# Last part of a vision tower: the first layer of each block with the tokens on the partitions, and four transpositions a step

## The chip, the cores and the metric

The kernel runs on one core of a Trainium2 chip. The core has five engines with a queue of their own each, which meet only through semaphores: TensorE (PE; its weight loads are shown as PEld), VectorE (DVE), ScalarE (ACT), GpSimd (POOL) and SyncE (SP), which only issues DMAs here. The metric is the device time of one execution in microseconds (us).

## The reference

A vision tower with 1,216 tokens of 256 features, in the kernel ten tiles of 128 tokens (the last is half full): patch embedding, attention, a mixture of experts, an integer attention, and last a residual network of three blocks. Only the last is touched:

```python
h = x
for blk in range(3):
    i0, i1 = (2 * blk, 2 * blk + 1)
    y = _qlora_linear(h, qweights[i0], scales[i0], biases[i0], lora_a[i0], lora_b[i0])
    y = _layernorm(y, ln_gamma[blk], ln_beta[blk])
    y = jax.nn.gelu(y, approximate=False)
    y = _qlora_linear(y, qweights[i1], scales[i1], biases[i1], lora_a[i1], lora_b[i1])
    h = y + h
```

`_qlora_linear` is `x @ w.T + bias` with a 256x256 matrix in float32 (the low rank term is added into it earlier), and `_layernorm` takes the mean off, divides by the root of the variance over the 256 features of a token, and applies gamma and beta.

## The kernel before

All of it is one program with every instruction and every wait written out; nothing is reordered. The last part (`ffn_tensor`, `ffn_scalar`, `ffn_vector`, `ffn_pool`) runs 15 steps: three blocks of five chunks, four chunks of 256 tokens and one of 192 (the short chunk, steps 4, 9 and 14). Step n is chunk n % 5 of block n // 5. Ahead of the steps, tiles of normed tokens are turned by TensorE (`turned`, L2323) and copied to SBUF by ScalarE (`entered`, L2400) into `ffn_xT`, which holds the features on the partitions; tiles 4 to 9 are interleaved with steps 0 to 2.

The weights of the first layer have been centred along their outputs, so that the mean of y is taken off by the product, and the bias likewise. A step before the change:

- `first` (PE, L2337): four products into `psum`, outputs on the partitions, tokens along the row.
- `squared` (ACT): two squares (L2410) and two copies with bias (L2412) out of `psum`, into `ffn_sq` and `ffn_y`.
- `joined` (DVE, L2266): adds the two halves of the squares.
- `summed` (PE, L2346): two products with a column of ones add up the squares over the partitions.
- `variance` (DVE, L2261), then a power of -1/2 on GpSimd (L2311) into `ffn_rs`.
- `spread` (PE, L2354): two products put that factor, one for each token, on all partitions.
- `normed` (DVE, L2273): multiplies y by it. `gelu` (ACT, L2420): two Gelus with gamma and beta.
- `second` (PE, L2370; in the last block L2376 and L2378, which end with the tokens on the partitions), and `added` (DVE, L2282; in the last block L2289, L2291 and L2292), which adds the residual.

In steps 5 to 9 GpSimd also adds the last bias to `h` (L2314), right behind its power. The order on TensorE is i = 0, 1, 2, ...: `first(i)`, (while i < 3: two `turned`), `summed(i-1)`, `spread(i-2)`, `second(i-3)`. In float32 one product of the program is two MATMUL instructions in the trace, a transposition is one. Names in the rows are memory regions: `ring` holds `ffn_y` and `ffn_sq`, `experts` holds the weights and `ffn_xT`, `tab` the identity and the ones, `shared` the last bias.

## Time and profile before

| | |
|---|---|
| time, median of 3 runs | 561.8 us (560.23 to 562.18) |
| the profiled execution's own time, and its span | 560.42 us, 558.6 us |
| busy in the span: PE, PEld, DVE, ACT, POOL | 419.3, 308.4, 317.6, 247.1, 143.7 us |
| mean granted TensorE clock | 0.841 of 2.4 GHz |
| the 15 steps on PE (first L2337 to last L2378) | 483.2 to 555.0 us |

The span is from the first to the last instruction; the execution's time lies 1.8 us above it. "Busy" adds up instructions; what an engine's idle time costs is told by the chain of work that ended last. The granted clock of TensorE is 1.00 (2.4 GHz) or 0.50 (1.2 GHz) in a stretch.

### The profile page before, as it was taken

The page shows a single profiled execution, that of the slowest core. Times are in us where ns is not written, and L with a number is a line of the kernel's source. Part 1 is how long each engine was busy: PE and PEld are TensorE (multiplying, and loading weights), DVE is VectorE, ACT ScalarE, POOL GpSimd, SP SyncE. Part 2 cuts the span into 40 slices and gives each one's busy share as a digit, 9 for nine tenths or more (in the row PEclk, how much of TensorE's full clock was granted, in tenths as well). Part 3 has the DMA queues.
Part 4 walks back from the last instruction along what each step waited for, and adds up shares of the span by engine and source line. Part 5 has one row for each costly group of instructions (what it writes and reads, how often), then busy time and mean ns, then how long its engine had stood idle before and what let it go on. Part 6 is the DMA issues. An engine that isn't in the chain of part 4 may idle for free.

```text
span 558.6 us, 9536 instructions
## 1 busy us (share of the span) xinstructions
PE 419.3 (75%) x3508; PEld 308.4 (55%) x3509; DVE 317.6 (57%) x867; ACT 247.1 (44%) x518; POOL 143.7 (26%) x169
## 2 busy tenths in 40 slices
PE   4777785468778999999889994632794235799997
PEld 3545562246568885666555793321442233589996
DVE  3858875489855421223311128669898975645642
ACT  4235543336656411222222212693396665385661
POOL 3644443069911240000000054008010001113410
PEclk9969987559999999999999998575556555599999
DMA  8921111096004222111101071000000000000002
GB/s 296 404 105 19 17 18 19 14 397 284 4 1 193 84 101 86 48 47 39 58 19 39 29 287 51 0 1 3 2 0 0 2 5 1 2 0 1 1 19 72
DMA packets 19793, 38.64 MB, mean 69 GB/s; under 512 B 2136, under 2 KB 16164, under 8 KB 18340
## 3 DMA queue, kind: packets, MB, share of 16 engines
q1 hardware_dynamic: 18788, 35.41, 18.3%
q0 software_dynamic: 960, 2.62, 1.4%
q8 instruction: 29, 0.48, 0.4%
q14 instruction: 16, 0.13, 0.1%
HBM read 29.77 MB, written 7.01 MB: 66 GB/s over the span
## 4 chain that ended last, share of the span: by engine, by line
PE 52%; DVE 24%; ACT 10%; issue 6%; POOL 6%; DMA 1%; SPq 0%; DVEq 0%; ACTq 0%
PE psum L1255 11%; PE psum L1262 6%; PE psum L1287 5%; PE psum L2337 4%; PE psum L1301 3%; PE psum L2370 3%; POOL ring L782 3%; POOL experts L787 2%; PE psum L610 2%; PE psum L2376 2%; PE psum L1279 1%; ACT experts L1663 1%; PE psum L2354 1%; DMA experts<-in_tern 1%; DVE ring L1939 1%
## 5 line engine op out<-in xcount | busy, mean ns | idle before, releaser
L1255 PE MATMUL psum<-experts,ring 128*128 x136 | 64.3, 596 | 1.9 <-issue 1.2
L1079 DVE TENSOR_TENSOR ring<-ring,psum 128x512 f32<-128x512 f32 x17 | 11.7, 688 | 62.8 <-PE psum L1255 62.8
L1186 POOL DMA_INDIRECT front<-expert_results,slot_of x10 | 9.9, 992 | 125.0 <-DMA expert_results<-ring 122.2
L1262 PE MATMUL psum<-front,shared 128*128 128x256 f32 (+1 forms) x160 | 34.6, 370 | 0.0
L1255 PEld LDWEIGHTS psum<-experts,ring 128*128 128x128 f32 x136 | 23.3, 190 | 19.4 <-issue 19.4
L1287 PE MATMUL psum<-experts,ring 128*128 x136 | 32.1, 379 | 0.0
L1287 PEld LDWEIGHTS psum<-experts,ring 128*128 128x128 f32 x136 | 25.8, 190 | 10.3 <-issue 7.6
L1262 PEld LDWEIGHTS psum<-front,shared 128*128 128x128 f32 x160 | 29.2, 190 | 3.2
L1385 ACT COPY ring<-psum 128x512 f32<-128x512 f32 x17 | 10.0, 586 | 42.3 <-PE psum L1279 42.3
L2337 PE MATMUL psum<-experts 128*128 128x256 f32 (+1 forms) x120 | 28.6, 384 | 0.0
L590 PE MATMUL psum<-experts,ring 128*128 128x256 f32 x108 | 25.9, 391 | 0.4 <-DVE experts L485 0.4
L1371 ACT COPY ring<-psum 128x256 f32<-128x256 f32 x17 | 6.3, 372 | 42.8 <-PE psum L1271 42.8
L782 POOL TENSOR_TENSOR ring<-ring,att_max 128x608 f32<-128x608 f32 x16 | 19.3, 1209 | 20.0 <-DVE att_max L849 19.2
L2337 PEld LDWEIGHTS psum<-experts 128*128 128x128 f32 x120 | 23.0, 200 | 2.7
L814 PE MATMUL psum<-tab,experts 128*128 128x128 f32 x128 | 18.8, 295 | 7.5 <-ACT ring L876 7.4
L1301 PE MATMUL psum<-shared,ring 128*128 128x256 f32 (+1 forms) x80 | 20.0, 406 | 4.5 <-issue 4.5
L618 PE MATMUL psum<-tab,ring 128*128 128x128 f32 x30 | 6.7, 343 | 22.0 <-DVE ring L451 22.0
L590 PEld LDWEIGHTS psum<-experts,ring 128*128 128x128 f32 x108 | 20.8, 199 | 3.7 <-DVE experts L485 0.6
L2111 POOL TENSOR_TENSOR rstd<-out_var,minus_half 128x2 f32<-128x2 f32 x5 | 4.2, 832 | 70.5 <-DVE out_var L2091 70.5
L2311 POOL TENSOR_TENSOR ffn_rs<-ffn_var,minus_half 128x2 f32<-128x2 f32 x15 | 10.4, 693 | 45.2 <-DVE ffn_var L2261 45.2
L2410 ACT ACTIVATE ring<-psum,ffn_first_b 128x256 f32<-128x256 f32 (+1 forms) x30 | 12.3, 459 | 20.5 <-PE psum L2337 20.5
L610 PE MATMUL psum<-qkv_w,ring 128*128 128x384 f32 x40 | 20.4, 647 | 1.1 <-DVE qkv_w L496 1.1
(364 smaller groups left out, 1076.0 us busy)
## 6 DMA issues: line engine op xcount, KB each, us to landing
experts<-in_experts SPq DMA_DIRECT2D x8, 1536.0 KB, 12.8
experts<-in_x SPq DMA_DIRECT2D x9, 384.0 KB, 8.2
expert_rows<-zeros SPq DMA_DIRECT2D x1, 2176.0 KB, 15.0
ring<-expert_rows SPq DMA_DIRECT2D x17, 128.0 KB, 2.1
shared<-in_shared SPq DMA_DIRECT2D x1, 1536.0 KB, 18.1
experts<-in_ffn_q SPq DMA_DIRECT2D x1, 1536.0 KB
experts<-in_ffn_s SPq DMA_DIRECT2D x1, 1536.0 KB
experts<-in_pos_embed SPq DMA_DIRECT2D x1, 1152.0 KB, 8.7
```

The source lines that it names most:

```text
L590: mm = nc.tensor.matmul(psum[:, Y, 0:D], tok_xT[t % 2][:, k, :], patch_c[:, k, :], start=(k == 0), stop=(k == KP - 1))
L610: mm = nc.tensor.matmul(psum[:, Z, 0:QKV], qkv_hT[t % 2][:, k, :], qkv_w[:, k, :], start=(k == 0), stop=(k == KD - 1))
L782: nc.gpsimd.tensor_tensor(att_s[p % 3], att_s[p % 3], m, ALU.subtract).then_inc(s_shifted.sem, 1)
L814: tr = nc.tensor.transpose(psum[:, 4 + c // 4, (c % 4) * P:(c % 4 + 1) * P], att_p[p % 3][:, 2 * c:2 * c + 2, :], ident)
L1079: nc.vector.tensor_tensor(o, o, up_bank(g), ALU.mult).then_inc(hidden_done.sem, 1)
L1255: mm = nc.tensor.matmul(bank, sl_xT[t % 2][:, k, :], slot_w(t, block, k, F), start=(k == 0), stop=(k == KD - 1))
L1262: mm = nc.tensor.matmul(o[:, b, 0:w], shared_w(block, k, (2 * half + b) * P, P), moe_x(c)[:, k, 0:w], start=(k == 0), stop=(k == KD - 1))
L1287: mm = nc.tensor.matmul(psum[:, 2, 0:D], sl_hT[t % 2][:, k, :], slot_w(t, 2, k, D), start=(k == 0), stop=(k == KF - 1))
L1301: mm = nc.tensor.matmul(psum[0:m, 3, u * D:(u + 1) * D], sh_h[c % 2][:, k, u * P:u * P + m], shared_w(2, k, 0, D), start=(k == 0), stop=(k ...
L2337: mm = nc.tensor.matmul(psum[:, n % 2, o * CHUNK:o * CHUNK + w], ffn_w[:, 2 * b, k, o * P:(o + 1) * P], ffn_xT[:, k, a:a + w], start=(k == ...
L2370: mm = nc.tensor.matmul(psum[:, 6 + n % 2, o * CHUNK:o * CHUNK + w], ffn_w[:, 2 * b + 1, k, o * P:(o + 1) * P], g[:, k, 0:w], start=(k == ...
L2410: nc.scalar.activation(ffn_sq[n % 2][:, k, 0:w], psum[:, n % 2, k * CHUNK:k * CHUNK + w], ACT.Square, bias=ffn_first_b[:, b, k:k + 1])
```

## The change

The first layer is computed with the tokens on the partitions, so that the squares of a token add up along its row. Line numbers of the changed kernel differ by some 10 to 20.

- `first` (now L2356): the tokens are the stationary side, and the 256 outputs the moving one, in all chunks.
- `biased` (new, DVE, L2277): adds a centred bias row, out of `psum` into `ffn_yt`, 128 x 512 at once (two instructions for the short chunk).
- `squared` (ACT, L2417): one Square of each tile out of `ffn_yt`, with its sum along the row.
- `variance` (DVE, L2285) adds the epsilon only; the power on GpSimd stays.
- `normed` (DVE, L2291): one multiplication of each tile by its column of `ffn_rs`, in SBUF.
- `y_turned` (new, PE, L2367): four transpositions into `psum`. `gelu` (ACT, L2427) reads them there.
- `joined`, `summed`, `spread` and the two copies with bias are gone.
- The pipeline has a stage less: `first(i)`, `y_turned(i-1)`, `second(i-2)`.
- Three bias rows are fetched behind the last bias (SP), and GpSimd takes the mean off them (L1882) behind the two memsets at L1874 and L1875.

```diff
+            for b in range(FFN_BLOCKS):
+                sp.dma_start(ffn_rows[:, b, :], ins["ffn_rows"][2 * b:2 * b + 1, :].to_broadcast((P, D))).then_inc(l_ffn_last.sem, 16)
...
+            pool.wait_ge(ffn_bias_ready.sem, ffn_bias_ready.done(0))
+            pool.wait_ge(l_ffn_last.sem, l_ffn_last.all)
+            for b in range(FFN_BLOCKS):
+                w = nc.gpsimd.tensor_scalar(ffn_rows[:, b, :], ffn_rows[:, b, :], ffn_mean[:, b:b + 1], None, ALU.add)
...
+            def biased(n):
+                dve.wait_ge(ffn_first.sem, ffn_first.done(n))
+                if n >= 3:
+                    dve.wait_ge(ffn_y_turned.sem, ffn_y_turned.done(n - 3))
+                z = psum[:, n % 2, :].rearrange("p (u d) -> p u d", u=2)
+                for m, u in parts(n):
+                    w = nc.vector.tensor_tensor(ffn_yt[n % 3][0:m, u, :], z[0:m, u, :],
+                                                ffn_rows[0:m, n // NC:n // NC + 1, :].to_broadcast((m, u.stop - u.start, D)), ALU.add)
...
             def normed(n):
-                w = FFN_CHUNKS[n % NC][1]
-                y = ffn_y[n % 4][:, :, 0:w]
-                dve.wait_ge(ffn_spread.sem, ffn_spread.done(n))
-                rs = psum[:, 4 + n % 2, 0:w].rearrange("p (o c) -> p o c", o=1).to_broadcast((P, KD, w))
-                nc.vector.tensor_tensor(y, y, rs, ALU.mult).then_inc(ffn_normed.sem, 1)
+                dve.wait_ge(ffn_rs_ready.sem, ffn_rs_ready.done(n))
+                for u, (_, m) in enumerate(tiles_of_chunk(n % NC)):
+                    y = ffn_yt[n % 3][0:m, u, :]
+                    w = nc.vector.tensor_scalar(y, y, ffn_rs[0:m, n % 2, u:u + 1], None, ALU.mult)
+                w.then_inc(ffn_normed.sem, 1)
...
-            for i in range(STEPS + 4):
-                if 0 <= i - 4 < STEPS:
-                    added(i - 4)
-                if 0 <= i - 1 < STEPS:
-                    variance(i - 1)
-                if 0 <= i - 2 < STEPS:
-                    normed(i - 2)
+            for i in range(STEPS + 3):
+                if 0 <= i - 3 < STEPS:
+                    added(i - 3)
+                if 0 <= i - 1 < STEPS:
+                    normed(i - 1)
                 if i < STEPS:
-                    joined(i)
+                    biased(i)
+                    variance(i)
...
-                for o in range(KD):
+                for u, (t, m) in enumerate(tiles_of_chunk(c)):
                     for k in range(KD):
-                        mm = nc.tensor.matmul(psum[:, n % 2, o * CHUNK:o * CHUNK + w], ffn_w[:, 2 * b, k, o * P:(o + 1) * P], ffn_xT[:, k, a:a + w],
+                        mm = nc.tensor.matmul(psum[0:m, n % 2, u * D:(u + 1) * D], ffn_xT[:, k, t * P:t * P + m], ffn_w[:, 2 * b, k, :],
...
+                        tr = nc.tensor.transpose(bank[:, k, u * P:u * P + m], ffn_yt[n % 3][0:m, u, k * P:(k + 1) * P], ident[0:m, 0:m])
...
+                    y = nc.scalar.activation(ffn_sq[n % 2][0:m, u, :], ffn_yt[n % 3][0:m, u, :], ACT.Square, scale=D ** -0.5, accum_out=ffn_mean_sq[0:m, n % 2, u:u + 1])
...
-            for i in range(STEPS + 2):
+            for i in range(STEPS + 1):
                 if i < STEPS:
                     squared(i)
                 if i < 3:
                     entered(4 + 2 * i)
                     entered(5 + 2 * i)
-                if 0 <= i - 2 < STEPS:
-                    gelu(i - 2)
+                if 0 <= i - 1 < STEPS:
+                    gelu(i - 1)
```

The semaphores of this part are those of earlier parts under new names, and the order shows the old ones: `gate_done` is `ffn_first`, `sl_hT_ready` is `ffn_rs_ready`, `sl_y_ready` is `ffn_normed`, `sh_down` is `ffn_gelu`, `sh_added` is `ffn_second`, `sl_hidden_turned` is `ffn_xT_ready`, `sl_xT_ready` is `ffn_turned`, `silu_done` is `ffn_squared`, `hidden_done` is `ffn_var_ready`, and `sl_down` is `ffn_spread` before and `ffn_y_turned` in the changed kernel.

TensorE before, from the end of `first(3)` to `first(4)`:

```order
L2337 MATMUL psum<-experts 128x256 x3
L2346 MATMUL psum<-tab,ring 128x1 [waits hidden_done,ffn_joined]
L2346 MATMUL psum<-tab,ring 128x1
L2354 MATMUL psum<-tab,ffn_rs 128x128 [waits sl_hT_ready]
L2354 MATMUL psum<-tab,ffn_rs 128x128
L2370 MATMUL psum<-ring,experts 128x256 [waits sl_hidden_turned,sh_down]
L2370 MATMUL psum<-ring,experts 128x256 x3
L2337 MATMUL psum<-experts 128x192 [waits silu_done,sl_hidden_turned]
L2337 MATMUL psum<-experts 128x192 x3
```

And TensorE in the changed kernel, from `y_turned(1)` to the first half of `first(4)`:

```order
L2367 MATMUL psum<-tab,ring 128x128 [waits sl_y_ready]
L2367 MATMUL psum<-tab,ring 128x128 x3
L2382 MATMUL psum<-ring,experts 128x256 [waits sl_hidden_turned,sh_down]
L2382 MATMUL psum<-ring,experts 128x256 x3
L2356 MATMUL psum<-experts 128x256 [waits ffn_biased,sl_hidden_turned]
L2356 MATMUL psum<-experts 128x256 x3
L2367 MATMUL psum<-tab,ring 128x128 [waits sh_down,sl_y_ready]
L2367 MATMUL psum<-tab,ring 128x128 x3
L2382 MATMUL psum<-ring,experts 128x256 [waits sl_hidden_turned,sh_down]
L2382 MATMUL psum<-ring,experts 128x256 x3
L2356 MATMUL psum<-experts 128x256 [waits ffn_biased,sl_hidden_turned]
L2356 MATMUL psum<-experts 128x256
```

`second(0)` (L2370, now L2382) stood ahead of `first(4)` and stands ahead of `first(3)` now; between two steps there is one wait on VectorE's result where there were two.

VectorE in a step of the changed kernel, from `variance(n-1)` to `biased(n)`:

```order
L2285 TENSOR_SCALAR ffn_var<-ffn_mean_sq 128x2 [waits sl_hT_ready,silu_done]
L2301 SCALAR_TENSOR_TENSOR experts<-psum,ffn_cols,experts 128x256 [waits sh_added]
L2301 SCALAR_TENSOR_TENSOR experts<-psum,ffn_cols,experts 128x256
L2291 TENSOR_SCALAR ring<-ring,ffn_rs 128x256 [waits sl_hT_ready]
L2291 TENSOR_SCALAR ring<-ring,ffn_rs 128x256
L2277 TENSOR_TENSOR ring<-psum,shared 128x512 [waits sl_down,gate_done]
```

`normed` waits for GpSimd's power of the same step, stands behind `added` of two steps earlier, and `biased` stands behind it.

ScalarE while the steps start, in the changed kernel, from `entered(4)` and `entered(5)` (L2410) to `squared(2)` and `entered(8)`:

```order
L2410 COPY experts<-psum 128x2x128 [waits sl_xT_ready] x2
L2417 ACTIVATE ring,ffn_mean_sq<-ring 128x256 [waits ffn_biased]
L2417 ACTIVATE ring,ffn_mean_sq<-ring 128x256
L2410 COPY experts<-psum 128x2x128 [waits sl_xT_ready] x2
L2427 ACT_TABLE_LOAD
L2427 ACTIVATE ring<-psum,ffn_cols 128x256 [waits sl_down]
L2427 ACTIVATE ring<-psum,ffn_cols 128x256
L2417 ACTIVATE ring,ffn_mean_sq<-ring 128x256 [waits hidden_done,ffn_biased]
L2417 ACTIVATE ring,ffn_mean_sq<-ring 128x256
L2410 COPY experts<-psum 128x2x128 [waits sl_xT_ready] x2
```

The copies of tiles 8 and 9 now stand behind `gelu(0)`; before, they stood ahead of it.

## Rows read from the trace of the kernel before

**Rows 1.** Chain that ended last, a step in steady state: start us, us, what

```profile
519.08 1.30 PE psum L2337 x8
520.38 0.34 PE psum L2346 x4
520.72 0.55 PE psum L2354 x4
521.27 1.73 PE psum L2370 x8
523.00 1.73 PE psum L2337 x8
```

**Rows 2.** The same chain, while the steps start

```profile
486.72 0.44 PE psum L2323 x4
...
493.76 1.28 ACT L2420
...
496.20 1.99 PE psum L2370 x8
```

**Rows 3.** Timeline, PE's next group and `added` behind a `second`

```profile
501.95 1.89 PE L2337 MATMUL psum<-experts 128*128 128x256 f32 x8
502.16 0.88 DVE L2282 SCALAR_TENSOR_TENSOR experts<-psum,ffn_cols,experts 128x256 f32<-128x256 f32 x2 [0.77 <-PE psum L2370]
```

**Rows 4.** Timeline, DVE and POOL in one step (start us, us, [idle before <-releaser])

```profile
525.10 0.16 DVE L2261 TENSOR_SCALAR ffn_var<-psum 128x2 f32<-128x2 f32 x1 [1.17 <-PE psum L2346]
525.34 0.69 POOL L2311 TENSOR_TENSOR ffn_rs<-ffn_var,minus_half 128x2 f32<-128x2 f32 x1 [2.41 <-DVE ffn_var L2261]
...
525.65 0.69 DVE L2273 TENSOR_TENSOR ring<-ring,psum 128x512 f32<-128x512 f32 x1 [0.40 <-PE psum L2354]
525.99 1.27 POOL L2314 TENSOR_TENSOR h<-h,shared 128x512 f32<-128x512 f32 x1
526.37 1.18 DVE L2266 TENSOR_TENSOR ring<-ring 128x256 f32<-128x256 f32 x1
```

**Rows 5.** ACT: timeline at 407.7 us, then groups by line (busy, mean ns)

```profile
407.72 0.36 ACT L2226 ACTIVATE experts<-psum 128x256 f32<-128x256 f32 x1
407.98 0.19 ACT L2226 ACTIVATION_READ_ACCUMULATOR experts<-psum 128x1 f32 x1
...
L2234 ACT ACTIVATE experts<-experts,lora_mean 128x256 f32<-128x256 f32 x5 | 2.1, 495 | 0.0
```

**Rows 6.** Timeline, DVE, an earlier part of the kernel

```profile
259.05 0.61 DVE L1500 TENSOR_SCALAR front<-front,w_inv 128x256 f32<-128x256 f32 x2
```

**Rows 7.** Timeline, ACT and DVE behind `first(0)`

```profile
486.76 0.84 ACT L2410 ACTIVATE ring<-psum,ffn_first_b 128x256 f32<-128x256 f32 x2 [2.77 <-PE psum L2337]
...
487.05 0.73 DVE L2098 TENSOR_SCALAR ring<-h,hst,rstd 128x256 f32<-128x256 f32 x2 [1.42 <-PE psum L2323]
...
488.20 0.66 ACT L2400 COPY experts<-psum 128x256 f32<-128x256 f32 x2
488.36 0.42 DVE L2266 TENSOR_TENSOR ring<-ring 128x256 f32<-128x256 f32 x1 [0.57 <-ACT ring L2412]
```

**Rows 8.** Timeline, POOL and DVE at 377 us

```profile
376.96 1.73 POOL L2242 TENSOR_SCALAR experts<-experts 128x512 f32<-128x512 int32 x2 [28.24 <-ACT experts L1723]
...
377.05 1.17 DVE L1646 TENSOR_SCALAR front<-experts 128x1152 bf16<-128x1152 f32 x1
```

**Rows 9.** Stretches: us, busy PE PEld DVE ACT POOL, granted clock, DMA share, GB/s

```profile
63.07:66.48 3.41, 1.80 (x9) 1.22 (x10) 3.16 (x16) 1.14 (x3) 1.00 (x2) 1.00 0.20 19
...
69.90:73.31 3.41, 1.36 (x7) 0.96 (x7) 3.12 (x17) 1.06 (x4) 0.55 (x1) 1.00 0.28 30
73.31:76.72 3.41, 3.41 (x12) 2.58 (x11) 2.60 (x9) 2.78 (x9) 2.63 (x5) 0.50 0.02 5
```

**Rows 10.** Timeline, PE in the stretch at 69.9 us

```profile
72.03 0.55 PE L618 MATMUL psum<-tab,ring 128*128 128x128 f32 x3 [2.05 <-DVE ring L451]
```

**Rows 11.** Timeline, POOL behind its memsets

```profile
468.06 0.81 POOL L2111 TENSOR_TENSOR rstd<-out_var,minus_half 128x2 f32<-128x2 f32 x1 [57.35 <-DVE out_var L2091]
```

More of the change, by code:

```diff
@@ L1429, in tower @@
         ffn_last = view(shared, 0, D)
+        ffn_rows = view(shared, D, FFN_BLOCKS, D)
         ffn_q = view(experts, 0, 3072).bitcast(I32)
@@ L2176, in tower @@
         ffn_mean = sb("ffn_mean", [P, B])
-        ffn_first_b = sb("ffn_first_b", [P, B, KD])
+        ffn_mean_sq = sb("ffn_mean_sq", [P, 2, 2])
+        ffn_yt = [view(ring, 4096 + u * 2 * D, 2, D) for u in range(3)]
         lora_sum = sb("lora_sum", [P, B, KD])
@@ L2257, in variance @@
             def variance(n):
[L2258 removed]
+                dve.wait_ge(ffn_squared.sem, ffn_squared.done(n))
                 if n >= 2:
                     dve.wait_ge(ffn_rs_ready.sem, ffn_rs_ready.done(n - 2))
[L2261 to L2266 removed]
@@ L2333, in first, with y_turned @@
                 if n >= 2:
-                    pe.wait_ge(ffn_squared.sem, ffn_squared.done(n - 2))
-                for o in range(KD):
+                    pe.wait_ge(ffn_biased.sem, ffn_biased.done(n - 2))
+                for u, (t, m) in enumerate(tiles_of_chunk(c)):
                     for k in range(KD):
-                        mm = nc.tensor.matmul(psum[:, n % 2, o * CHUNK:o * CHUNK + w], ffn_w[:, 2 * b, k, o * P:(o + 1) * P], ffn_xT[:, k, a:a + w],
+                        mm = nc.tensor.matmul(psum[0:m, n % 2, u * D:(u + 1) * D], ffn_xT[:, k, t * P:t * P + m], ffn_w[:, 2 * b, k, :],
                                               start=(k == 0), stop=(k == KD - 1))
                 mm.then_inc(ffn_first.sem, 1)
-            def summed(n):
-                pe.wait_ge(ffn_joined.sem, ffn_joined.done(n))
+            def y_turned(n):
+                pe.wait_ge(ffn_normed.sem, ffn_normed.done(n))
                 if n >= 2:
-                    pe.wait_ge(ffn_var_ready.sem, ffn_var_ready.done(n - 2))
-                for u in range(2):
-                    mm = nc.tensor.matmul(psum[:, 2 + n % 2, u:u + 1], ffn_sq[n % 2][:, 0, u * P:(u + 1) * P], ones[:, 0:1], start=True, stop=True)
-                mm.then_inc(ffn_summed.sem, 1)
-            def spread(n):
-                pe.wait_ge(ffn_rs_ready.sem, ffn_rs_ready.done(n))
-                if n >= 2:
-                    pe.wait_ge(ffn_normed.sem, ffn_normed.done(n - 2))
+                    pe.wait_ge(ffn_gelu.sem, ffn_gelu.done(n - 2))
+                bank = psum[:, 4 + n % 2, :].rearrange("p (k c) -> p k c", k=KD)
                 for u, (_, m) in enumerate(tiles_of_chunk(n % NC)):
-                    mm = nc.tensor.matmul(psum[:, 4 + n % 2, u * P:u * P + m], ffn_rs[:, n % 2, u:u + 1].to_broadcast((P, P)), ident[:, 0:m],
-                                          start=True, stop=True)
-                mm.then_inc(ffn_spread.sem, 1)
+                    for k in range(KD):
+                        tr = nc.tensor.transpose(bank[:, k, u * P:u * P + m], ffn_yt[n % 3][0:m, u, k * P:(k + 1) * P], ident[0:m, 0:m])
+                tr.then_inc(ffn_y_turned.sem, 1)
             def second(n):
@@ L2383, in ffn_tensor @@
                 turned(t)
-            for i in range(STEPS + 3):
+            for i in range(STEPS + 2):
                 if i < STEPS:
@@ L2390, in ffn_tensor @@
                 if 0 <= i - 1 < STEPS:
-                    summed(i - 1)
+                    y_turned(i - 1)
                 if 0 <= i - 2 < STEPS:
-                    spread(i - 2)
-                if 0 <= i - 3 < STEPS:
-                    second(i - 3)
+                    second(i - 2)
         def ffn_scalar(act):
```

48 lines of the change are left out of this document (22 added, 26 removed).

## The prediction

> **What bounds the kernel now.** I read the chain of work that ended last first. From 498.2 us to the end of the last product it is TensorE alone, product behind product: a full step is `summed` 0.34, `spread` 0.55, `second` 1.73 and `first` 1.73 us, 4.35 together; in the short chunk `first` and `second` take 1.30 each [rows 1]. In the last block `second` is longer, and the chain is TensorE's just the same. So in these 57 us every microsecond of TensorE counts, and the other engines have slack. Before 498.2 the steps fill up: TensorE waits once, some 0.8 us, for ScalarE's table load (1.28) and first Gelus, and `second(0)` starts at 496.20 [rows 2]. The reader is to see that the change takes work from the bounding engine, and lengthens the loop that runs through the others.
>
> **TensorE's work.** Removed: 15 `summed` at 0.34 = 5.1, and 15 `spread` at 0.55 (some 0.50) = 8.1; together 13.2. Added: 15 times four transpositions. The same operation on the same shape is there: four in 0.44 [rows 2]; 12 full steps and 3 short ones at 0.33 make 6.3. `first` of the short chunk now moves 256 outputs for two tiles, 1.73 for 1.30, three times: 1.3. **Net -5.6 us.** If TensorE stayed the bound throughout, that would be the result.
>
> **The new chain of one step**, from the last product of `first(n)` to the first transposition of `y_turned(n)`:
>
> to VectorE: 0.20 from the start of TensorE's next group to an operation behind a product [rows 3]
>
> `biased`: 0.69, as the other sum of 128x512 out of `psum` [rows 4]; 0.04 on to ScalarE
>
> two squares with their accumulator reads: the trace has no such pair out of SBUF. Below: the pair out of `psum` (the read starts 0.26 behind its operation, the next operation 0.10 later: 0.36 apart; then 0.26 + 0.19) gives 0.81 [rows 5]. Above: two of 0.495 end to end with two reads of 0.19 give 1.37. An SBUF operation of 256 takes 0.495 against 0.36 [rows 5], overlapped as that pair: 0.49 to the second start, then 0.39 + 0.19: **1.07**
>
> 0.04, `variance` 0.16, 0.08 to 0.17 on to GpSimd (525.10 + 0.16 to 525.34), power 0.69 [rows 4], 0.10 back to VectorE (my estimate, between the hand-overs of 0.04 and 0.17)
>
> `normed`: 0.61 for two, the second 0.27 behind the first, as the two multiplications of 128x256 by a column [rows 6]; 0.05 to TensorE.
>
> That is 3.82. On TensorE there stand between the same two points `y_turned(n-1)` 0.44, `second(n-2)` 1.73, `first(n+1)` 1.73: 3.90. So in steady state without disturbance the chain is just hidden. The other loop is hidden as closely: behind a `second`, VectorE needs 0.20, `added` 0.81 to its release (0.88 less the overlap) [rows 3], `normed` 0.61 and 0.05, 1.67 against the 1.73 of the `first` that stands between. Before, two hand-overs with separate slots shared this latency, and VectorE never had more than 1.2 us of it in one slot.
>
> **Where it isn't hidden**, in four places, and the clock.
>
> *The start.* By hand, from the moment VectorE is free at 487.7 (487.05 + 0.73) [rows 7]: `biased(0)` to 488.4, where ScalarE read `psum` directly at 486.76 [rows 7]. Squares to 489.5; the copies of tiles 4 and 5 (0.66 for two [rows 7]) stand behind them, so `turned(6)` starts at 489.9: TensorE, done with `first(1)` and nothing else to do since 488.7, idles 1.1. The rest of the chain ends at 491.3: 1.0 idle before `y_turned(0)`. `first(2)` to 493.5. `biased(1)` 491.2, squares to 493.0, copies 6 and 7 to 493.6; `y_turned(1)` at 494.8: 0.9 idle. ScalarE goes on in its order: table load 1.28 to 494.8 [rows 2], `gelu(0)` some 1.0 (two operations of 0.5, as the one in SBUF [rows 5]) to 495.9, squares(2) to 496.9, copies 8 and 9 to 497.5, and `second(0)` waits for tile 9: it starts at 497.5, after 2.3 idle. Sum 5.3 against 0.8: **+4.5**. `second(0)` starts 1.3 later than before, with one `first` less done.
>
> *Steps 5 to 9.* GpSimd starts its 1.27 us addition as the power ends (525.99 against 525.34 + 0.69), and `joined`, issued at 526.37, ends at 527.55 [rows 4], though it takes 0.42 where GpSimd is idle [rows 7]: it began about 1.14 behind GpSimd's start. `joined` reads two tensors in SBUF. `normed` reads one, but a one-tensor operation was held too: 1.17 us for 1152 elements beside GpSimd [rows 8]. Now `normed` is released by just that power, so each of the five comes up against the addition. From the start of `biased` to the next: 0.69 + 0.04 + 1.07 + 0.04 + 0.16 + 0.17 + 0.69 = 2.86, then 1.10 held, then 0.53 to issue `normed`: 4.49 for a step, against 3.90. The first of them is late by 0.9 (3.82 + 1.10 less the 3.90), four by 0.6, and the one that has the short `second(4)` beside it by 0.4 more: 3.7; with `biased` in two pieces in step 9 (0.1), **+3.8**. That makes these steps slower than before (4.35), not quicker.
>
> *The end.* `normed(14)` stands behind `added(12)`, and no `first` hides it any more: 0.20, 0.62 for the sum (0.69 [rows 4] less the overlap), 0.61 and 0.05 = **+1.5** idle. Before, this slot was full.
>
> *The rest.* Behind `second(9)`, 0.43 shorter than a full one, the chain of 3.82 sticks out by 0.35, and each idle time adds about 0.1 to load weights (1.99 against 1.73 includes that and the last product's latency [rows 1, 2]) where it is not itself inside a longer loop: **+0.6**.
>
> Sum: -5.6 + 4.5 + 3.8 + 1.5 + 0.6 = **+4.8**.
>
> *The clock.* Nearly all of the last part runs at 2.4 GHz. Between 493.5 and 497.5 TensorE would have only two transpositions of tiles and `y_turned(1)`, 0.7 to 0.9 us of work around an idle time of 2.3. In 69.90 to 73.31 it was busy 1.36 us, and ran at 1.2 GHz from 73.31 to 76.72; in 63.07 to 66.48, busy 1.80, it kept 2.4 [rows 9]. The first of these held an idle time of 2.05 [rows 10]. The new start is nearer to the first. A stretch as long as that one at half speed, TensorE being busy in 2.6 us of it, costs 1.3; a second one costs 1.7 more. I take **+2.7**, with 0 and 3.5 as bounds.
>
> Hidden: the three bias rows' DMAs go out behind the last load of SyncE before the outputs, and nothing on it waits for them in between. GpSimd's three sums (up to 0.6 each, as L2242 [rows 8]) fit into the 57.35 us it idles behind its memsets [rows 11]; a hold on VectorE by them, were it not covered, would cost at most 1.8. VectorE's and ScalarE's totals fall and bound nothing.
>
> The profiled execution took 560.42: 560.4 + 4.8 + 2.7 = 567.9. The median of the runs stands 1.4 higher, so I say **568.3 us**.
>
> **The rivals.**
>
> *The clock stays* (0.25). 560.4 + 4.8 = 565.2. For it: TensorE is never idle for more than 2.3 us in one piece at the start, and it kept its clock behind a stretch in which it was idle for 1.6 of 3.4 us [rows 9]. Against it: it has less work here than in either. The Trainium skill (TensorE: Matmul & The Clock Gate, section "HAM oscillation — how this bites in real kernels") ties the fall to an idle gap of TensorE that by its figure is longer than any worked out here; by that rule the clock stays, and the time is this rival's. The trace disagrees with the rule: the fall at 73.31 came behind an idle time of 2.05 us.
>
> *`normed` is not held by GpSimd* (0.15). 3.8 goes: 564.1 with the fall, 561.4 without. Against it: the operation at 377.05 [rows 8], a single case with another output type. The Trainium skill (SBUF — State Buffer, section "Who interferes with whom") describes a port that the two engines lock against each other; by it `normed` is held and this rival is out.
>
> *Faster* (0.05): the chain through ScalarE is much shorter than I size it, and TensorE stays the bound. The place is the pair of squares and all that waits on it: three of the idle times at the start and the hold in steps 5 to 9 (which is inside a loop with the squares). Each 0.1 us less for the pair saves about 0.9 in all; at the lower end, 0.81, the sum is +2.4, and 562.8 without the fall of the clock. It decides for faster from 0.23 for the pair on (4.8 less 7.6 is -2.8, 557.6 us); the trace has no single ScalarE operation of 256 elements under 0.36 [rows 5].
>
> *Slower still* (0.10): squares at 1.37, +2.7 more, or the clock falls a second time at the end: 570.5 to 573.
>
> The likeliest as worked out: 0.45, own range 566.5 to 570.
>
> **How the numbers follow.** 0.5% (2.8 us) is about what a measurement of this kernel can tell from no change. Slower by more: the likeliest, the clock rival (+4.8), the slower one, and the held-free case with the fall (+3.7): 0.45 + 0.25 + 0.10 + 0.10, less 0.06 for mis-sizing, 0.84. Within: the held-free case without the fall and that 0.06: 0.11. Faster: 0.05. The range leaves out the faster case, the held-free one without the fall and the end of the slowest: 562.5 to 572.5.
>
> **What would show it.** In the profile of the changed kernel: `y_turned` at 0.44 and no more; idle of TensorE before L2367 put down to VectorE, in steps 5 to 9 about 0.6 to 1.0 each and almost none in steps 2 to 4; L2291 at 1.4 to 1.7 us for two in steps 5 to 9 and 0.61 elsewhere; L2382 first at 497.5, released by ScalarE's copy; a granted clock of 0.50 just behind; 1.5 idle before the last L2367. I am wrong if steps 5 to 9 are 3.9 long, if the start is shorter, or if the pair of squares isn't near 1.07.

## The result, and the profile after

The changed kernel took **564.6 us** (median of 17 runs, 561.5 to 569.1) against 560.4 for the one before (17 runs, 556.1 to 562.2): ratio 1.0090, 95% interval 1.0060 to 1.0119. Taken again (12 runs) it was 1.0051, 1.0022 to 1.0080. By the two ratios it is slower by 2.9 and 5.0 us, by their intervals by 1.2 to 6.7. The profiled execution took 561.69 us, with a span of 559.9 and a mean granted clock of 0.857. Of the profiles below, that of "last norm first" is of a slow execution (568.45 us, the kernel's median is 560.9), so only the rows of its last part are used, and not its time.

Of the page after, the row of busy times (419.3 on PE before, 143.7 on POOL, 247.1 on ACT):

```profile
PE 414.5 (74%) x3449; PEld 298.2 (53%) x3449; DVE 319.7 (57%) x885; ACT 235.0 (42%) x518; POOL 146.6 (26%) x172
```

TensorE does less, as the change means it to, and the kernel takes longer. (Part of the 4.8 us is the clock: the row of `first(0)`, which ran at the lower clock for a while, is 3.35 us before and 2.16 here.) VectorE's total is not smaller but larger, 319.7 for 317.6. The chain of work that ended last says why: while the steps start it is ScalarE's rows above all, and in steps 5 to 9 VectorE's stand in it, where [rows 1] are TensorE alone.

```profile
486.27 0.92 ACT ring L2417 x4
490.97 1.28 ACT L2427
493.18 0.90 ACT ring L2417 x4
494.76 1.97 PE psum L2382 x8
...
509.85 0.98 DVE ring L2291 x2
511.53 1.32 PE psum L2382 x8
513.53 1.10 DVE ring L2291
```

Timeline of PE while the steps start, in steps 5 and 6, and at the end (start us, us, [idle before <-releaser]); it answers to [rows 2]:

```profile
482.42 2.16 PE L2356 MATMUL psum<-experts 128*128 128x256 f32 x8
...
487.58 0.69 PE L2342 MATMUL psum<-tab,ring 128*128 128x128 f32 x4 [0.84 <-ACT experts L2410]
488.95 0.66 PE L2367 MATMUL psum<-tab,ring 128*128 128x128 f32 x4 [0.68 <-DVE ring L2291]
...
492.10 0.66 PE L2367 MATMUL psum<-tab,ring 128*128 128x128 f32 x4 [0.33 <-DVE ring L2291]
494.76 1.97 PE L2382 MATMUL psum<-ring,experts 128*128 128x256 f32 x8 [2.00 <-ACT experts L2410]
...
510.87 0.66 PE L2367 MATMUL psum<-tab,ring 128*128 128x128 f32 x4 [0.21 <-DVE ring L2291]
...
515.04 0.66 PE L2367 MATMUL psum<-tab,ring 128*128 128x128 f32 x4 [0.48 <-DVE ring L2291]
...
550.01 0.70 PE L2367 MATMUL psum<-tab,ring 128*128 128x128 f32 x4 [1.30 <-DVE ring L2291]
```

The waits stand at the start, in steps 5 to 9 and at the end, where the prediction put them, with the releasers that it gave them; in steps 7 and 8 no idle time is listed. Two things help in reading such rows. A full group whose row is 1.89 is followed by the next one 1.73 after its start where nothing is waited for. So a row reaches 0.16 into its follower, and an idle time in brackets begins 0.16 late: the 2.00 is 2.16. And lengths are best taken from start to start.

One chain of a step, timeline of ACT, DVE and POOL behind `first(0)`, where nothing else is in the way; it answers to [rows 4, 5, 7]:

```profile
486.27 0.42 ACT L2417 ACTIVATE ring<-ring 128x256 f32<-128x256 f32 x1 [3.24 <-DVE ring L2277]
486.60 0.19 ACT L2417 ACTIVATION_READ_ACCUMULATOR ring<-ring 128x1 f32 x1
486.69 0.40 ACT L2417 ACTIVATE ring<-ring 128x256 f32<-128x256 f32 x1
486.99 0.19 ACT L2417 ACTIVATION_READ_ACCUMULATOR ring<-ring 128x1 f32 x1
...
487.21 0.17 DVE L2285 TENSOR_SCALAR ffn_var<-ffn_mean_sq 128x2 f32<-128x2 f32 x1 [0.97 <-ACT ring L2417]
...
487.55 0.69 POOL L2330 TENSOR_TENSOR ffn_rs<-ffn_var,minus_half 128x2 f32<-128x2 f32 x1 [3.04 <-DVE ffn_var L2285]
...
488.27 0.62 DVE L2291 TENSOR_SCALAR ring<-ring,ffn_rs 128x256 f32<-128x256 f32 x2 [0.89 <-POOL ffn_rs L2330]
```

The pair of squares takes 0.91 (486.27 to 487.18).

And step 5, where GpSimd adds the last bias:

```profile
508.48 0.69 POOL L2330 TENSOR_TENSOR ffn_rs<-ffn_var,minus_half 128x2 f32<-128x2 f32 x1 [3.30 <-DVE ffn_var L2285]
...
508.98 0.87 DVE L2301 SCALAR_TENSOR_TENSOR experts<-psum,ffn_cols,experts 128x256 f32<-128x256 f32 x2 [0.57 <-PE psum L2382]
...
509.13 1.27 POOL L2333 TENSOR_TENSOR h<-h,shared 128x512 f32<-128x512 f32 x1
509.77 1.05 DVE L2291 TENSOR_SCALAR ring<-ring,ffn_rs 128x256 f32<-128x256 f32 x2
```

`normed` takes 1.05 for 0.61. It began 0.64 behind the addition, since `added` stood ahead of it on VectorE. In the five steps it takes 1.05, 1.45, 0.90, 1.02 and 1.09.

**One length for all kernels below** is that of the last part, from the start of `first(0)` to the end of the last product. The clock rises to 1.00 somewhere in `first(0)` or just ahead of it, differently in each execution: its row is 1.89 to 3.56 long, and that alone is worth up to 1.7 us. So I take off what the row of `first(0)` has over the 1.89 of a full one ("at full clock"). Before: 483.37 to 555.00, 71.6, with 3.35 for `first(0)`: **70.2**. After: 482.42 to 556.28, 73.9, with 2.16: **73.6**. The change costs 3.4 us there. The correction is good to some 0.2 us: in the second profile of the changed kernel the row of `first(0)` is 1.89, and its last part, less a fall of the clock told below, is 73.8. There `biased(0)` (485.63) stood behind VectorE's last multiplications of tokens (484.34 and on, without idle time), so that an earlier end of `first(0)` won nothing.

### The profile page after: what moved, and what is told of

Read it like the earlier page. It is cut to its first block, busy times and chain, and to the rows that moved or that the text cites. A ratio compares the mean times of both kernels' runs of the same rounds, so it can differ in the third digit from the quotient of the medians.

```text
span 559.9 us, 9452 instructions
## 1 busy us (share of the span) xinstructions
PE 414.5 (74%) x3449; PEld 298.2 (53%) x3449; DVE 319.7 (57%) x885; ACT 235.0 (42%) x518; POOL 146.6 (26%) x172
## 4 chain that ended last, share of the span: by engine, by line
PE 52%; DVE 27%; ACT 10%; issue 7%; POOL 2%; DMA 1%; SPq 0%; DVEq 0%; POOLq 0%; ACTq 0%
PE psum L1257 11%; PE psum L1264 6%; PE psum L1289 5%; PE psum L1303 3%; PE psum L2382 3%; PE psum L2356 3%; PE psum L2222 2%; PE psum L2221 2%; DVE ring L846 2%; DVE att_den L853 2%; PE psum L2388 2%; PE psum L610 1%; PE psum L2367 1%; PE psum L1281 1%; DVE att_max L849 1%
## 5 line engine op out<-in xcount | busy, mean ns | idle before, releaser
L1264 PE MATMUL psum<-front,shared 128*128 128x256 f32 (+1 forms) x160 | 36.1, 381 | 0.0
L1264 PEld LDWEIGHTS psum<-front,shared 128*128 128x128 f32 x160 | 30.4, 198 | 3.5
L2356 PE MATMUL psum<-experts 128*128 128x256 f32 (+1 forms) x120 | 29.1, 383 | 0.0
L2417 ACT ACTIVATE ring<-ring 128x256 f32<-128x256 f32 (+1 forms) x30 | 12.2, 408 | 36.1 <-DVE ring L2277 36.1
L2356 PEld LDWEIGHTS psum<-experts 128*128 128x128 f32 (+1 forms) x120 | 21.8, 188 | 3.9 <-issue 1.0
L1084 DVE TENSOR_TENSOR ring<-ring,psum 128x512 f32<-128x512 f32 (+1 forms) x10 | 6.6, 660 | 25.4 <-PE psum L1264 25.2
```

The lines of the kernel that those rows point to most:

```text
L1264: mm = nc.tensor.matmul(o[:, b, 0:w], shared_w(block, k, (2 * half + b) * P, P), moe_x(c)[:, k, 0:w], start=(k == 0), stop=(k == KD - 1))
L2356: mm = nc.tensor.matmul(psum[0:m, n % 2, u * D:(u + 1) * D], ffn_xT[:, k, t * P:t * P + m], ffn_w[:, 2 * b, k, :], start=(k == 0), stop=(k ...
L2417: y = nc.scalar.activation(ffn_sq[n % 2][0:m, u, :], ffn_yt[n % 3][0:m, u, :], ACT.Square, scale=D ** -0.5, accum_out=ffn_mean_sq[0:m, n % ...
```

## The experiments

| kernel | last part as it ran | at full clock | ratio to before (95%) |
|---|---|---|---|
| before, twice | 71.6, 71.6 | 70.2, 70.2 | 1 |
| changed, twice | 73.9, 75.5 | 73.6, 73.8 (fall taken off) | 1.0090 and 1.0051 |
| addition early | 72.1 | 71.7 | 1.0058 (1.0024 to 1.0091) |
| copies first | 74.0 | 72.3 | 1.0046 (1.0013 to 1.0080) |
| second later | 74.4 | 73.0 | 1.0036 (1.0001 to 1.0071) |
| last norm first | 75.3 | 72.5 (fall taken off) | 1.0030 (0.9997 to 1.0063) |
| three edits together | 70.8 | 69.3 | 1.0012 (0.9980 to 1.0045) |
| more room | 71.6 | 71.2 | 1.0016 (0.9978 to 1.0053) |
| third square | 76.6 | 76.1 | 1.0111 (1.0060 to 1.0161) |
| one stage more | 67.4 | 67.0 | 0.9937 (0.9905 to 0.9969) |
| and the table early | 66.5 | 66.1 | 0.9917 (0.9885 to 0.9950) |
| and full tiles | 65.8 | 65.3 | 0.9907 (0.9876 to 0.9937) |

Each ratio is to the runs of the kernel before that were taken beside it. The intervals are 3 to 4 us wide, that of the third square (4 runs) 5.7. Single edits are told apart by the profiles, and only the larger sums by the times.

### The changed kernel again, and the clock

> The changed kernel once more, to see whether its profile repeats and as the reference for the kernels beside it. Both theories of the clock: if the fall at the start that was predicted belongs to the kernel, a second profile shows a granted clock of 0.50 somewhere in 486 to 502 us and the time of this run is 2 to 3 us above 561.7; if it doesn't (or depends on the execution), the start runs at 1.00 as in the first profile, the idle times before second(0) are again 0.8, 0.7, 0.3, 2.0, and the kernel stays 3 to 5 us slower than the one before.

The idle times were there again, and this time the clock fell. Stretches (us, busy PE PEld DVE ACT POOL, granted clock), then PE's timeline:

```profile
492.18:495.59 3.41, 1.40 (x8) 1.12 (x9) 0.72 (x2) 3.40 (x11) 0.69 (x1) 1.00 0.00 0
495.59:499.00 3.41, 3.41 (x10) 2.69 (x9) 1.08 (x4) 0.04 (x1) 0.00 (x0) 0.50 0.00 0
```
```profile
494.85 3.03 PE L2382 MATMUL psum<-ring,experts 128*128 128x256 f32 x8 [2.00 <-ACT experts L2410]
497.67 2.55 PE L2356 MATMUL psum<-experts 128*128 128x256 f32 x8
500.06 0.60 PE L2367 MATMUL psum<-tab,ring 128*128 128x128 f32 x4
```

From the start of `second(0)` to `y_turned(2)` it is 5.21 us for 3.53: the fall costs 1.7. It is the fall that was predicted, in the stretch where it was put. Of the five profiles whose start is that of the changed kernel (both of its own, addition early, last norm first, more room) it came in two, here and in "last norm first" (3.43 for `second(0)`, +1.5), while every one of the five has the idle time of 2.00. So it depends on the execution. My estimate from these five is 0.6 us on average (1.7 and 1.5, divided by five), not 2.7; two falls in five are too few for more than that. The kernel before, looked at a second time, has its idle time of 0.66 ahead of `second(0)` again, and a granted clock of 1.00 from there to the end, as in its first profile.

### The addition early

```diff
             for n in range(STEPS):
+                if NC <= n < 2 * NC:
+                    pool.wait_ge(ffn_first.sem, ffn_first.done(n))
+                    nc.gpsimd.tensor_tensor(h[...], h[...], ffn_last..., ALU.add)
                 pool.wait_ge(ffn_var_ready.sem, ffn_var_ready.done(n))
...
-                if NC <= n < 2 * NC:
-                    nc.gpsimd.tensor_tensor(h[...], h[...], ffn_last..., ALU.add)
```

> In steps 5 to 9 GpSimd's addition now runs beside biased and squares, not beside normed. Theory (normed is held by GpSimd's addition): L2291 goes from 0.90 to 1.45 for two back to 0.61, the five steps go from 4.17 to 4.37 down to 3.9 to 4.05, and the time falls by 1.2 to 2.2 us against the changed kernel; biased may be held a little instead, by at most 0.3 in a step. Rival (the five steps are long because the chain through ScalarE is longer than TensorE's work): L2291 changes, the steps keep 4.1 to 4.3, time within 0.5 us.

DVE and POOL in step 5 of it:

```profile
509.37 0.60 DVE L2291 TENSOR_SCALAR ring<-ring,ffn_rs 128x256 f32<-128x256 f32 x2
510.30 0.69 DVE L2277 TENSOR_TENSOR ring<-psum,shared 128x512 f32<-128x512 f32 x1 [0.34 <-PE psum L2357]
```
```profile
510.34 1.27 POOL L2330 TENSOR_TENSOR h<-h,shared 128x512 f32<-128x512 f32 x1 [1.43 <-PE psum L2357]
```

`normed` is back at 0.60 to 0.62 in all five steps, and no idle time of TensorE is left in them. The period ahead of `y_turned(5)` is 4.13 against 4.50, and those from it on are 3.52, 3.95, 4.13, 3.95 and 4.13, against 4.17, 4.17, 4.29, 4.37 and 4.19 (3.9 to 4.05 were expected; the short chunks scatter them). The last part is 1.9 shorter. `biased`, which now begins beside the addition, takes 0.69 as ever: it reads `psum` and one tensor in SBUF. In the time the difference can't be seen (1.0058).

### The copies first

```diff
-                if i < STEPS:
-                    squared(i)
                 if i < 3:
                     entered(4 + 2 * i)
                     entered(5 + 2 * i)
+                if i < STEPS:
+                    squared(i)
```

> ScalarE copies tiles 4 to 9 ahead of the squares of steps 0 to 2. Theory (second(0) is late because ScalarE's copy of tile 9 stands behind three pairs of squares): the idle of 2.0 before the first L2382 shrinks to 0.9 to 1.2, where gelu(0) bounds it, and TensorE reaches the end 0.7 to 1.3 us earlier, less up to 0.6 that y_turned(0) and y_turned(1) lose because their squares now stand behind copies: 0.3 to 1.0 us faster than the changed kernel. Rival (the start is bound by the table load and gelu(0), whatever the copies do): second(0) within 0.2 us of where it was, no gain.

```profile
491.15 0.66 PE L2367 MATMUL psum<-tab,ring 128*128 128x128 f32 x4 [1.77 <-DVE ring L2291]
...
494.31 0.66 PE L2367 MATMUL psum<-tab,ring 128*128 128x128 f32 x4 [0.34 <-DVE ring L2291]
495.65 1.97 PE L2382 MATMUL psum<-ring,experts 128*128 128x256 f32 x8 [0.68 <-ACT experts L2410]
```

The 2.00 ahead of `second(0)` is 0.68, and the last part is 1.3 shorter, both beyond what was expected (0.9 to 1.2, and 0.3 to 1.0). It was the copy of tile 9 behind the squares. `y_turned(0)` and `y_turned(1)` lost nothing by the copies ahead of their squares: less the excess of `first(0)`, `y_turned(0)` starts 6.26 us after `first(0)` in both kernels, and `y_turned(1)` 3.16 after that (3.15 in the changed kernel).

### Second later

```diff
-                if 0 <= i - 2 < STEPS:
-                    second(i - 2)
+                if 0 <= i - 3 < STEPS:
+                    second(i - 3)
```
(TensorE; `added(i - 4)` on VectorE)

> second and added move one step later, so that first(3) stands ahead of second(0) again, as in the kernel before, and one more slot stands between the last y_turned and the last second. Theory (the missing stage costs the idle time at the start and at the end): the 2.0 before the first L2382 is filled by first(3), the step at the end keeps at most 0.7 of the 1.3 idle before the last L2367; sum 1.5 to 2.5 us faster than the changed kernel. Rival (the order with more distance only shifts the idle time: first(5) then waits for added(0), which now comes one step later): an idle time of 0.5 or more appears before L2356 in each step, and the kernel is 2 us slower or more.

```profile
499.53 0.66 PE L2367 MATMUL psum<-tab,ring 128*128 128x128 f32 x4 [1.26 <-DVE ring L2291]
```

0.6 us was won, not 1.5 to 2.5. `second(0)` is off the start, but `y_turned(2)` waits 1.26 in its place: its squares (496.96) stand behind ScalarE's table load and `gelu(0)`. And the end is as it was: 1.30. My reason for the end was wrong in its form. `added` moved along with `second`, so `normed(14)` still stands behind an `added` whose `second` TensorE does last before it wants `normed(14)`.

### The last norm first

```diff
             for i in range(STEPS + 3):
+                if i == STEPS:
+                    normed(i - 1)
                 if 0 <= i - 3 < STEPS:
                     added(i - 3)
-                if 0 <= i - 1 < STEPS:
+                if 0 <= i - 1 < STEPS - 1:
                     normed(i - 1)
```

> VectorE's normed(14) stands ahead of added(12) instead of behind it; nothing else moves. Theory (the 1.30 idle before the last L2367 is normed(14) standing behind added(12), which waits for second(12)): now only the chain from first(14) bounds it, 3.5 us against 3.06 us of products beside it, so the idle becomes 0.4 to 0.5, and the last part 0.8 to 0.9 us shorter. Rival (the chain from first(14) through ScalarE and GpSimd sets it): idle 1.2 or more, nothing won.

```profile
556.77 0.70 PE L2369 MATMUL psum<-tab,ring 128*128 128x128 f32 x4 [0.18 <-DVE ring L2291]
```

0.18 for 1.30 (0.4 to 0.5 was expected), and the last part 1.1 shorter at full clock (0.8 to 0.9): the wait at the end was the place in VectorE's queue. The periods of its steps are those of the changed kernel to 0.02, but for the fall of the clock and the end.

### Three edits together

The early addition, the copies first and the last norm first.

> The early addition, the copies first and the last norm first, together. Theory (the three places are independent): TensorE from the first y_turned to the end is shorter than in the changed kernel (67.3) by 1.9 + 1.3 + 0.8, so 63.2 to 63.5 us where the clock doesn't fall, no idle before L2367 but in the start and 0.4 to 0.5 at the end, and the time is 3.5 to 4.2 us under the changed kernel, within 1 us of the kernel before on either side. Rival (what is taken from one wait reappears in the next): 65 us or more.

It held but for 0.2: from the first `y_turned` to the end 63.0 us (494.89 to 557.92), 67.3 in the changed kernel. At the end 0.19 is left. The gains add up: 73.6 less 1.9, 1.3 and 1.1 is 69.3, as measured. The median is 559.7 us, beside 559.4 of the kernel before: level with it.

### More room

```diff
+                if 3 <= i < STEPS:
+                    second(i - 2)
                 if 0 <= i - 1 < STEPS:
                     y_turned(i - 1)
-                if 0 <= i - 2 < STEPS:
+                if 0 <= i - 2 < STEPS and not 3 <= i < STEPS:
                     second(i - 2)
```

> In steps 3 to 14 TensorE does second(i-2) ahead of y_turned(i-1), so 1.7 us more of its work stands between first(n) and y_turned(n); GpSimd's addition stays where it was. Theory (the hold costs time only because the chain of a step has no slack): normed is still held (L2291 0.9 us or more for two in steps 5 to 9, up to 1.9), but TensorE idles less than 0.3 us in all before L2367 from step 3 to 13, and the last part is 1.2 to 2.2 us shorter than in the changed kernel, for the most part what the early addition gave. Rival (TensorE is bound in these steps by something else, VectorE's own loop): periods of 4.2 to 4.4 stay in steps 5 to 9.

POOL and DVE in step 6 of it:

```profile
514.64 1.26 POOL L2333 TENSOR_TENSOR h<-h,shared 128x512 f32<-128x512 f32 x1
514.71 1.61 DVE L2291 TENSOR_SCALAR ring<-ring,ffn_rs 128x256 f32<-128x256 f32 x2 [0.17 <-POOL ffn_rs L2330]
```

Here `normed` meets the addition at its start and is held in full, five times at 1.60 or 1.61 for 0.61. TensorE doesn't wait for it once from step 3 to 13, and the last part is 2.4 shorter than in the changed kernel (1.2 to 2.2 was expected): 0.4 of it is at the end, where 0.86 is left of the 1.30, and the other 1.9 is as much as the early addition gave. So the hold itself cost nothing here; it costs what the chain has no slack for.

### A third square

```diff
+                nc.scalar.activation(psum[:, 2 + n % 2, 0:D], ffn_yt[n % 3][:, 0, :], ACT.Square, scale=D ** -0.5)
                 for u, (_, m) in enumerate(tiles_of_chunk(n % NC)):
```
(one square more, whose result is used nowhere)

> ScalarE does one more square of 128x256 ahead of each pair, about 0.40 us, 15 times; it adds nothing to TensorE's work. Theory (the chain through the squares sets the start and the steps 5 to 9, and has 0.3 to 0.4 us of slack in the others): second(0) 1.2 us later (three pairs stand ahead of the copy of tile 9), steps 5 to 9 0.3 to 0.4 longer each, steps 2 to 4 and 10 to 13 at most 0.2 longer, the end 0.0 to 0.1: 2.8 to 4.2 us slower than the changed kernel in the last part. Rival (ScalarE isn't on the path but in the start): 1.2 us slower. With the longer idle times at the start the clock has more reason to fall there: a stretch at 0.50 behind second(0) adds 1.8.

```profile
512.42 0.66 PE L2367 MATMUL psum<-tab,ring 128*128 128x128 f32 x4 [0.51 <-DVE ring L2291]
...
516.89 0.66 PE L2367 MATMUL psum<-tab,ring 128*128 128x128 f32 x4 [0.78 <-DVE ring L2291]
```

0.40 us more for ScalarE in each step made the last part 2.5 longer (2.8 to 4.2 was expected), 0.9 of it ahead of `second(0)` and 1.6 behind it, though TensorE's work is the same. That is 0.6 for each 0.1, where I had said 0.9. What lies behind `second(0)` is in steps 5 to 9 (periods from `y_turned(5)` on 4.47, 4.48, 4.47, 4.53, 4.19), in the one ahead (4.80 for 4.50) and the one behind (3.81 for 3.51); steps 2 to 4 still had the slack. The clock fell here too, at 490.4, behind `first(1)`, but in front of an idle time, and it cost little that can be told from the rest.

### One stage more, and the table early

```diff
-            for i in range(STEPS + 2):
+            for i in range(STEPS + 3):
...
-                if 0 <= i - 1 < STEPS:
-                    y_turned(i - 1)
-                if 0 <= i - 2 < STEPS:
-                    second(i - 2)
+                if 0 <= i - 2 < STEPS:
+                    y_turned(i - 2)
+                if 0 <= i - 3 < STEPS:
+                    second(i - 3)
```
(with `added(i - 4)`, and with the early addition and the copies first as above; the second kernel adds one line ahead of ScalarE's steps)
```diff
+            nc.scalar.activation(ffn_gelu_early[:, 0:1], ffn_mean[:, 0:1], ACT.Gelu)
```

> One stage more: y_turned two steps and second three steps behind first (added four), with the early addition and the copies first as before. Theory (the change loses by the waits at the start, in steps 5 to 9 and at the end; its products alone are 2.9 us shorter): with one first more ahead of y_turned(0) and of the last ones, TensorE idles only at the start, under 2.0 us in all, none from step 3 on, and none at the end; from first(0) to the last product it takes 67.5 to 68.5 us at full clock, against 73.6 in the changed kernel, 70.2 in the one before and 69.3 with the three edits. Time: 1.5 to 3 us under the kernel before, 5 us under the changed one. Rival (some 69 us is what TensorE's own work takes, with its weight loads and restarts): 69 us or more, no difference to the kernel before.

> The kernel with one stage more, and one Gelu of a single column on ScalarE ahead of the first squares, so that the table is loaded where ScalarE waits for VectorE anyway. Theory (the table load of 1.28 us stands on the chain to second(0)): second(0) starts 0.6 to 1.3 us earlier, and the last part is 0.6 to 1.3 us shorter than in the kernel with one stage more. Rival (the copies of tiles and the chain through VectorE set the start): within 0.2 us.

Timeline of PE, the start of the second of them:

```profile
492.56 1.97 PE L2358 MATMUL psum<-experts 128*128 128x256 f32 x8
495.03 0.66 PE L2369 MATMUL psum<-tab,ring 128*128 128x128 f32 x4 [0.51 <-DVE ring L2292]
495.53 1.89 PE L2384 MATMUL psum<-ring,experts 128*128 128x256 f32 x8
497.26 2.03 PE L2358 MATMUL psum<-experts 128*128 128x256 f32 x8
499.22 0.66 PE L2369 MATMUL psum<-tab,ring 128*128 128x128 f32 x4
```

With a stage more, TensorE idles 1.19 us in all (0.51 and 0.68), and with the table loaded in ScalarE's idle time before the first squares, 0.51. The last part is 67.0 and 66.1 (67.5 to 68.5, then 0.6 to 1.3 less, were expected), and the kernel beats the one before: 0.9937 and 0.9917. The change was sound, and the pipeline around it was too short. The same edits were not tried on the kernel before; its one wait is 0.66 and 0.16, so they could win it 0.8 us at most, which leaves 3.3 between 69.4 and 66.1.

Of the two moved operations only the copies do what they did before. `first(n)` now runs a stage further ahead and is done by the time GpSimd's power of step n-1 ends. So the addition starts right behind that power again, and `normed` is held in full in all five steps, 1.60 to 1.62, in both kernels. DVE, the second of them:

```profile
508.07 1.61 DVE L2292 TENSOR_SCALAR ring<-ring,ffn_rs 128x256 f32<-128x256 f32 x2
```

No idle time of TensorE is listed in these steps: the stage takes the hold too, as in "more room".

The second of them also weighs the first term of the sum by itself, since almost no waits are left: 66.1 less 0.51 and the 0.16, against 70.2 less the 0.66 and 0.16 before, is 65.4 against 69.4. **TensorE's own work falls by 4.0 us, not 5.6.**

### Full tiles

`first` and `y_turned` take the last tile of the short chunk with 128 tokens instead of 64 (`psum[:, ...]`, `ffn_xT[:, k, t * P:(t + 1) * P]`, and `ident` for `ident[0:m, 0:m]`). The results of the padding are used nowhere.

> The kernel with one stage more and the early table load; first and y_turned of the short chunk now take the last tile with all 128 tokens, as all the others, instead of 64 (the padding tokens' results are used nowhere). TensorE moves more columns and the same number of products. Theory (a change of the tile's size costs TensorE time: first(4) took 1.97 from its start to the next group, a full one 1.73; y_turned(4) 0.57 against 0.44; the second behind it 1.83 against 1.73): these three become 1.73, 0.44 and 1.73, so 0.45 us less in each of three steps, and the last part is 1.2 to 1.5 us shorter at full clock than 66.1; this is what the sum of TensorE's work missed. Rival (the 64-token tiles cost what they cost by their data, or the later group waits for VectorE's bias sum in two pieces): within 0.3 us of 66.1.

```profile
494.30 1.89 PE L2358 MATMUL psum<-experts 128*128 128x256 f32 x8
496.02 0.60 PE L2369 MATMUL psum<-tab,ring 128*128 128x128 f32 x4
...
503.81 0.60 PE L2369 MATMUL psum<-tab,ring 128*128 128x128 f32 x4
504.25 1.89 PE L2384 MATMUL psum<-ring,experts 128*128 128x256 f32 x8
505.97 1.89 PE L2358 MATMUL psum<-experts 128*128 128x256 f32 x8
```

Each price came out as expected. `first(4)` (494.30) has a slot of 1.72 where it had 1.96 (497.26 to 499.22 above); `y_turned(4)` (503.81) 0.44 for 0.58 with the table early, and `second(3)` behind it 1.72 for 1.83. More columns in less time, with all groups of one shape. VectorE's bias sum of the short chunk is still in two pieces (0.74 us for both at 498.26), so that rival is out. Only 0.8 of the 1.2 to 1.5 us was kept. `normed` is held in full in the five steps, as in the two kernels ahead, and VectorE then takes 4.17 us a step (`normed` starts at 505.10, 509.28, 513.45, 517.61), where TensorE would take 3.90. TensorE now comes so early that it runs into that (DVE, then POOL, then PE's weight loads of `first(10)`):

```profile
517.61 1.62 DVE L2292 TENSOR_SCALAR ring<-ring,ffn_rs 128x256 f32<-128x256 f32 x2
```
```profile
517.55 1.27 POOL L2331 TENSOR_TENSOR h<-h,shared 128x512 f32<-128x512 f32 x1
```
```profile
517.63 1.38 PEld L2358 LDWEIGHTS psum<-experts 128*128 128x128 f32 x7 [0.54 <-DVE experts L2302]
```

`first(10)` and `first(11)` start 0.29 and 0.24 late, behind `added` (L2302), and they and `first(9)` take 1.83 for 1.73: 0.8 in all. No run keeps the addition off `normed` in this pipeline, so what that would win stays open.

## Why the prediction was right, and where its sizes were off

The direction, the three places of the waits and the mechanism held, and the range held the time. The forecast of 568.3 was 3.7 and 4.8 above the two medians, and both lie under the likeliest case's own range of 566.5 to 570; the rival "the clock stays" had 565.2. (The rival "`normed` is not held" had 564.1 with the fall: as near by its number, and wrong in its mechanism.) The sum was +4.8 against 3.4 at full clock, and it is as near as that by luck: one term was 1.6 too favourable, the others 3.0 too dear together.

Two of my sums are wrong as well. The 567.9 and the 1.4 by which the median stood above the profiled execution make 569.3, not 568.3. And the first held step is late by 1.0 (3.82 + 1.10 less 3.90), not 0.9, so the term of the hold should have been +3.9. VectorE's total did not fall either.

Term by term:

- **TensorE's work: -5.6 said, -4.0 measured** (one stage more with the table early). This is the step of the sum that was most too favourable. `y_turned` is 0.43 to 0.49 and full `first` and `second` 1.73, as said; the miss is the short chunk. I put its `first` at 1.73 and its `y_turned` at 0.33; they took 1.96 and 0.57, and the `second` behind is 0.1 longer: 0.57 in each of three steps, 1.7 in all. The full tiles show the cause: it goes when the tile has 128 tokens, and it is not a wait.
- **The start: +4.5 said, +3.7 measured.** The idle times with their 0.16 are 1.00, 0.84, 0.49 and 2.16, 4.5 in all, less 0.8 before; I had 5.3. The place and the releasers were right: `second(0)` came when ScalarE had copied tile 9, and the copies first took that away. Less the excess of `first(0)`, `second(0)` came 0.7 later than before, where I had 1.3. 0.5 of the 0.8 by which I was over is the squares: 0.91 for the pair, where I took 1.07 between bounds of 0.81 and 1.37, three times over. The Square in SBUF takes 0.40 to 0.42, nearer to the `psum` operation of [rows 5] than to the SBUF one of 0.495, which also has a bias by column.
- **The hold in steps 5 to 9: +3.8 said, +1.9 measured** (the early addition). This is the term of the waits that failed most. The mechanism is right, and so is its full size, 1.00 (I had 1.10), but only where `normed` meets the addition's start, as in "more room". What failed is that each of the five meets the addition at its beginning: in the changed kernel `added` stands between the power and `normed`, and 0.3 to 0.85 us of the hold was left. I had that `added` in the order of the queue, and left it out of this step. The rival "`normed` is not held" is out; the rule of the Trainium skill that I cited (SBUF — State Buffer, "Who interferes with whom") agrees with the 1.61 for 0.61, and with the untouched 0.69 of `biased`: by it an operation of that kind with one input in SBUF doesn't meet GpSimd there, and a `tensor_scalar` from SBUF to SBUF can.
- **The end: +1.5 said, 1.46 measured** (1.30 and 0.16), with its cause shown by the last norm first.
- **The rest: +0.6 said.** 3.4 less the four others leaves 0.3. The 0.35 behind `second(9)` did not come: no idle time is listed there. That the quicker squares left the chain hidden is likely, but no run shows it by itself.
- **The clock: +2.7 said, 0 in the first profile and 1.7 in the second.** Both the likeliest case and the rival "the clock stays" happen, by the execution: the fall came in two of five profiles. A fall was priced as a certainty in the likeliest case, at more than it costs when it comes. The rule of the Trainium skill that I cited for the rival (TensorE: Matmul & The Clock Gate, "HAM oscillation — how this bites in real kernels") would have it never fall here. The runs disagree with it: the longest idle time ahead of the fall in the second profile is 2.00 us (2.16 from start to start).
- **The bias sums on GpSimd** took 0.92 each, where I had up to 0.6, at 410.9 to 413.7 us, in its long idle time. No run leaves them out; nothing in the profile shows a cost.

That is 3.4 us and about 0.6 for the clock, 4.0, between the 2.9 and 5.0 that the two ratios give.

Of the signs that I gave, the pair of squares (0.91), the held `normed` (0.90 to 1.45, where I had 1.4 to 1.7), the idle times in steps 5 to 9 (0.21 to 0.48 in three steps and none listed in two, where I had 0.6 to 1.0 each) and the start of `second(0)` (494.76 for 497.5) all came out on the small side. By "I am wrong if the start is shorter, or if the pair of squares isn't near 1.07", the sizes were wrong where the direction was right.

The "faster" rival named the right lever, the latency between `first` and `y_turned`, but the wrong way to pull it. A pair slower by 0.4 cost 0.6 us for each 0.1, not 0.9; a quicker pair was not run. One more stage, with the copies first and the table early, takes all but 0.5 us of the waits.

## What to carry to other kernels

When a change takes work off the bounding engine but lengthens the loop through the others, compare the loop with the work that stands beside it in the queue, and buy slack with a pipeline stage before judging the change: here the same products were 0.5 to 0.9% slower with a stage less, and 0.6 to 0.8% faster with a stage more, the tile copies first and the table loaded early. Look at the head of each in-order queue too, at the first and the last step above all: a copy behind squares, a norm behind the sum of an earlier step (`added`) and a table load were 1.3, 1.1 and 0.9 us. For a long hold between two engines, first ask which operation stands between their starts, and whether anything waits for its end. And look again at the hold after each other edit: the addition that had been moved off `normed` was back on it once `first` ran a stage further ahead.

## What the runs showed that I had not expected

- A 64-token tile among 128-token ones costs TensorE more than a full tile: 1.96 for 1.73 and 0.57 for 0.44, and 0.1 for the group behind.
- The same program with the same idle times keeps its clock in one execution and loses it in the next. Ahead of the three falls seen TensorE was busy for 1.40 us from 492.18 to 495.59 (the changed kernel), 1.50 from 497.33 to 500.74 (the last norm first) and 1.58 from 487.00 to 490.41 (the third square).
- A full hold of two VectorE operations by GpSimd's 1.27 us cost TensorE nothing where it had 1.7 us more work beside the chain, and nothing with a stage more, until the full tiles made TensorE's steps shorter than VectorE's 4.17.
